# Attention in a 16-block transformer kernel: the shift of the scores moves from a second product into a row of the query stack

## What is computed

```python
q = _split_heads(queries @ Wq, h)          # h = 16 heads of 16 features
k = _split_heads(keys @ Wk, h)
v = _split_heads(values @ Wv, h)
scores = jnp.einsum('bhqd,bhkd->bhqk', q, k) / jnp.sqrt(jnp.float32(dh))
attn = jax.nn.softmax(scores, axis=-1)
y = jnp.einsum('bhqk,bhkd->bhqd', attn, v)
```

## Time and profile before

| | us |
|---|---|
| median of 3 runs | 431.51 (430.98, 431.51, 434.98) |
| the profiled execution: its own time | 433.9 |
| its span, first to last instruction | 432.0 |
| TensorE busy / VectorE busy / ScalarE busy | 344.1 / 306.4 / 248.9 |
| projection stage, until the first line 1216 | 0 to 53 |
| attention stage | 53 to about 180 |
| feed-forward stage | about 180 to 300 |
| gates and the last two layers | 300 to 432 |

### The profile page before, as it was taken

The page is one execution under the profiler, slowest core; times in us unless marked ns, Lnnn a source line. Parts: engine busy times, 40 slices in busy tenths (PEclk is TensorE's granted clock), DMA queues, the critical chain, the costliest instruction groups (busy, mean ns, idle before and its releaser), DMA issues.

```text
span 432.0 us, 9170 instructions
## 1 busy us (share of the span) xinstructions
PE 344.1 (80%) x3130; PEld 244.1 (57%) x3137; DVE 306.4 (71%) x1028; ACT 248.9 (58%) x470; POOL 185.1 (43%) x209
## 2 busy tenths in 40 slices
PE   2995698989999999824667776677489999999775
PEld 2774566767677777502445554355356666666422
DVE  3897454778898987676999999951537777787641
ACT  1564424664545545726788988874446666666520
POOL 2115200121212345149999999971004555445520
PEclk9999869999999999955999999989579999999965
DMA  7499999988476540000000000000001122212000
GB/s 242 136 281 281 273 303 289 242 167 150 95 148 112 127 71 2 1 0 0 2 1 2 0 2 1 2 0 2 0 14 27 37 51 50 50 39 39 24 25 24
DMA packets 48045, 35.78 MB, mean 83 GB/s; under 512 B 20096, under 2 KB 44032, under 8 KB 47872
## 3 DMA queue, kind: packets, MB, share of 16 engines
q1 hardware_dynamic: 48000, 35.20, 34.1%
HBM read 26.80 MB, written 8.39 MB: 81 GB/s over the span
## 4 chain that ended last, share of the span: by engine, by line
PE 53%; DVE 17%; issue 12%; ACT 5%; POOL 5%; DMA 3%; SPq 3%; DVEq 0%; POOLq 0%; ACTq 0%
PE PS L1438 6%; PE PS L1227 4%; PE PS L1216 4%; PE PS L1246 4%; DVE sm L736 4%; PE PS L1285 4%; PE PS L1428 4%; PE PS L1207 4%; PE PS L1206 4%; PE PS L1405 3%; DMA scr_k<-kpart 3%; PE PS L1423 2%; ACT pT L990 2%; SPq L315 2%; DVE sm L712 2%
## 5 line engine op out<-in xcount | busy, mean ns | idle before, releaser
L990 ACT ACTIVATE pT<-PS 128x512 f32<-128x512 f32 x64 | 36.6, 596 | 49.5 <-PE PS L1207 49.3
L605 DVE TENSOR_REDUCE negm<-PS 128x4 bf16<-128x512 f32 x64 | 42.4, 684 | 15.5 <-PE PS L1216 15.4
L434 POOL TENSOR_TENSOR sm<-sm,mhalf 128x1 f32<-128x1 f32 x16 | 11.3, 708 | 93.0 <-DVE sm L637 93.0
L450 POOL TENSOR_TENSOR kst<-kst,rows 128x1024 f32<-128x1024 f32 x16 | 37.6, 2351 | 5.0 <-ACT kst L1055 4.9
L464 POOL TENSOR_TENSOR kst<-kst,rows 128x1024 f32<-128x1024 f32 x16 | 37.8, 2365 | 0.0
L1320 PE MATMUL PS<-identf,w2f 128*128 128x128 f32 x128 | 19.2, 298 | 23.2 <-ACT w2f L1044 23.0
L1207 PE MATMUL PS<-identb,negm 128*128 128x128 bf16 x256 | 35.6, 222 | 0.0
L1227 PE MATMUL PS<-pT,vx 128*32 128x128 f32 x512 | 27.3, 287 | 5.0 <-ACT pT L990 5.0
L1320 PEld LDWEIGHTS PS<-identf,w2f 128*128 128x128 f32 x128 | 15.1, 151 | 27.7 <-ACT w2f L1044 22.4
L1438 PE MATMUL PS<-wd,xT 128*128 128x392 f32 x64 | 27.7, 560 | 1.8 <-DVE rest L884 1.8
L484 POOL TENSOR_TENSOR smd<-smd,mhalf 128x1 f32<-128x1 f32 x16 | 8.8, 550 | 44.9 <-DVE smd L915 44.9
(11 more groups left out here) (225 smaller groups left out, 1002.6 us busy)
## 6 DMA issues: line engine op xcount, KB each, us to landing
scr_q<-qpart SPq DMA_DIRECT2D x8, 384.0 KB, 4.9
scr_k<-kpart SPq DMA_DIRECT2D x8, 384.0 KB, 6.0
rows<-in_rows SPq DMA_DIRECT2D x1, 2056.0 KB, 11.3
X<-in_x SPq DMA_DIRECT2D x8, 256.0 KB, 4.7
CTXT<-in_ctxT SPq DMA_DIRECT2D x8, 256.0 KB, 4.6
cTb<-in_ctxT SPq DMA_DIRECT2D x16, 128.0 KB, 4.3
vx<-in_ctx SPq DMA_DIRECT2D x16, 128.0 KB, 2.7
out<-rest SPq DMA_DIRECT2D x16, 128.0 KB, 1.7
```

The costliest lines, as they stand in the source:

```text
L450: gp.tensor_tensor(n2[q.slot], n2[q.slot], ln2g, ALU.mult).then_inc(b_g2, 1)
L605: v.tensor_reduce(negm[f.slot % 2][:, 4 * hg:4 * hg + 4], PS[:, 2 + hg % 2, :].rearrange("p (h k) -> p h k", h=4), AX_X, ALU.max, negate=T ...
L990: s.activation(pT[:, hg, :], PS[:, hg % 2, :], ACT.Exp, scale=float(DH0) ** -0.5).then_inc(a_e, 1)
```

## The change

One row is appended to each stack, on partition 96. In the key stack it is all ones, written once by VectorE as its first four instructions. In the query stack it is the row of negated maxima of all 16 heads. For it TensorE transposes `negm` (128 by 16) at the end of the turn in which the maxima are taken, ScalarE copies the 16 by 128 result to `negmT`, and SyncE writes it by DMA as one row of 2048 values (`write_shift_row`). `shifted` is then one product of 97 rows per head.

There is one stage more: v of a block is made in the turn behind its maxima (stage m), `shifted`, the exponentials and `pv` another turn later (b is block t-2), and c, d and e are one turn later too (t-3, t-4, t-5). The loop has a turn more. On TensorE the first group of `shifted` now stands ahead of the transposes of c, and the Wo product ahead of the last `pv`; on VectorE the maxima 0 and 1 and the statistics of d stand ahead of `normalise`. SyncE's stream is a row, the stacks of the block three further on, and then the weights. The stacks still wait for the block that had their slot, which is now read a turn later.

```diff
+        negmT = [sb(f"negmT{i}", [H0, S], BF16) for i in range(2)]
...
+            def write_shift_row(at):
+                sp.wait_ge(a_n, at.b + 1)
+                sp.dma_start(qst[at.slot][STACK:STACK + 1], negmT[at.slot % 2][:]).then_inc(a_row[at.slot % 2], 16)
+
+            for x in range(NB):
+                write_shift_row(Turn(x, x % 4, x // 4))
+                if 4 <= x + 3 < NB:
+                    load_stacks(Turn(x + 3, (x + 3) % 4, (x + 3) // 4))
+                if x < 4:
+                    load_weights(x)
...
+            for i in range(4):
+                last = v.memset(kst[i][STACK:STACK + 1], 1.0)
+            last.then_inc(a_ones, 1)
...
-            def turn_a(f, _b, c, d):
-                if c:
-                    normalise(c)
-                    if c.b == 3:
-                        weight_means()
+            def turn_a(f, _m, _b, c, d):
                 if f:
                     take_max(f, 0)
                     take_max(f, 1)
                 if d:
                     bn = ln1_stats(d)
+                if c:
+                    normalise(c)
+                    if c.b == 4:
+                        weight_means()
...
-                if c and 4 <= c.b < 10:
-                    ternary_step(c.b - 4)
-                if c and c.b == 10:
+                if c and 5 <= c.b < 11:
+                    ternary_step(c.b - 5)
+                if c and c.b == 11:
                     sum_weights()
...
                 if f:
+                    act.wait_ge(a_nt, f.b + 1)
+                    if f.b >= 2:
+
+                        act.wait_ge(a_row[f.slot % 2], f.b // 2 * 16)
+                    s.activation(negmT[f.slot % 2][:], PS[0:H0, 6, 0:64].bitcast(BF16), ACT.Copy).then_inc(a_n, 1)
+                    if f.b in (5, 6):
+                        weight_sum(f.b - 5)
...
-                    pe.wait_ge(a_mx, b.b * 4 + hg + 1)
+                    if hg == 0:
+                        pe.wait_ge(a_row[b.slot % 2], 16 * (b.b // 2 + 1))
                     done(pe, a_e, b, 0, 4, hg - 1)
                     for j in range(4):
                         h = 4 * hg + j
-                        block = PS[:, hg % 2, j * 128:(j + 1) * 128]
-                        t.matmul(block, kst[b.slot][0:STACK, h, :], qst[b.slot][0:STACK, h, :], start=True, stop=False)
-                        last = t.matmul(block, negm[b.slot % 2][:, h:h + 1].to_broadcast([128, 128]), identb[:],
-                                        start=False, stop=True)
+                        last = t.matmul(PS[:, hg % 2, j * 128:(j + 1) * 128], kst[b.slot][0:STACK + 1, h, :],
+                                        qst[b.slot][0:STACK + 1, h, :], start=True, stop=True)
                     last.then_inc(a_s2, 1)
...
+                if f:
+                    pe.wait_ge(a_mx, f.b * 4 + 4)
+                    done(pe, a_n, f, 0)
+                    t.transpose(PS[0:H0, 6, 0:64].bitcast(BF16), negm[f.slot % 2][:], identb[:]).then_inc(a_nt, 1)
```

More of the change, by code:

```diff
@@ L169, in build @@
         a_ld = [sem(f"a_stacks_loaded{i}") for i in range(4)]
-        a_s1 = sem("a_scores_for_max"); a_mx = sem("a_max_taken")
+        a_row = [sem(f"a_shift_row_written{i}") for i in range(2)]; a_ones = sem("a_ones_rows_ready")
+        a_s1 = sem("a_scores_for_max"); a_mx = sem("a_max_taken"); a_nt = sem("a_max_transposed"); a_n = sem("a_maxT_ready")
         a_s2 = sem("a_scores_shifted"); a_e = sem("a_exp_ready")
@@ L441, in _ @@
             pool.wait_ge(s_rows, 16)
-            pipeline(pool, NB, 4, 4, turn_a, tail=False)
+            for t in range(NB + 1):
+                turn_a(*peeled(t, NB, 4, 5))
             def turn_b(tau, _a, _b, p, q, _c, _d, e, _f, _g):
@@ L763, in turn_b @@
                     spreads(b, d, tau)
-            pipeline(dve, NB, 4, 4, turn_a, tail=False)
-            turn_a(*peeled(NB, NB, 4, 4))
+            for t in range(NB + 2):
+                turn_a(*peeled(t, NB, 4, 5))
             first, last, before_last = Turn(0, 0, 0), Turn(NB - 1, 3, 3), Turn(NB - 2, 2, 3)
@@ L994, in turn_a @@
                     exp(1)
+                if m:
+                    act.wait_ge(a_vm, m.b + 1)
+                    done(act, a_pv, m, -1, 4)
+                    s.activation(vx[m.slot % 2][:, :, 0:DH0], PS[:, 4, 0:256].rearrange("p (h e) -> p h e", h=H0),
+                                 ACT.Copy).then_inc(a_v, 1)
+                if b:
                     if b.b == NB - 1:
@@ L1008, in turn_a @@
                 if f:
[L1009 to L1014, removed]
+                    act.wait_ge(a_nt, f.b + 1)
[4 more added lines that the diff above has]
+                        weight_sum(f.b - 5)
                 if e:
                     level(e)
-            pipeline(act, NB, 4, 5, turn_a, tail=False)
+            for t in range(NB + 1):
+                turn_a(*peeled(t, NB, 4, 6))
             def gelu(b):
@@ L1229, in pv @@
                     last.then_inc(a_pv, 1)
+                if f:
+                    pe.wait_ge(a_ld[f.slot], LOADED * (f.used + 1))
+                    for_max(0)
+                    for_max(1)
+                if m:
+                    done(pe, a_v, m, 0)
+                    for kc in range(KC):
+                        last = t.matmul(PS[:, 4, 0:256], cTb[m.slot][:, kc, :], wv[:, kc, :],
+                                        start=(kc == 0), stop=(kc == KC - 1))
+                    last.then_inc(a_vm, 1)
+                if b:
+                    shifted(0)
                 if c:
@@ L1239, in turn_a @@
                         up(Turn(1, 1, 0))
-                if f:
-                    pe.wait_ge(a_ld[f.slot], LOADED * (f.used + 1))
-                    for_max(0)
-                    for_max(1)
-                    done(pe, a_v, f, 0)
-                    for kc in range(KC):
-                        last = t.matmul(PS[:, 4, 0:256], cTb[f.slot][:, kc, :], wv[:, kc, :],
-                                        start=(kc == 0), stop=(kc == KC - 1))
-                    last.then_inc(a_vm, 1)
                 if b:
-                    shifted(0)
                     shifted(1)
@@ L1253, in turn_a @@
                         columns(Turn(0, 0, 0))
+                    pv(0)
+                if f:
+                    for_max(2)
                 if c:
@@ L1257, in turn_a @@
                     done(pe, a_x, c, 0)
-                    if isinstance(c.b, int) and c.b == 3:
+                    if c.b == 4:
                         pe.wait_ge(s_wsum, 2)
@@ L1265, in turn_a @@
                     last.then_inc(a_t2, 1)
-                if b:
-                    pv(0)
-                if f:
-                    for_max(2)
                 if b:
@@ L1287, in turn_a @@
                     last.then_inc(a_o, 1)
-            pipeline(pe, NB, 4, 3, turn_a, head=8, tail=False)
+                if b:
+                    pv(3)
+                if f:
+                    pe.wait_ge(a_mx, f.b * 4 + 4)
+                    done(pe, a_n, f, 0)
+                    t.transpose(PS[0:H0, 6, 0:64].bitcast(BF16), negm[f.slot % 2][:], identb[:]).then_inc(a_nt, 1)
+            pe.wait_ge(a_ones, 1)
+            for i in range(NB + 1):
+                turn_a(*peeled(i, NB, 4, 4))
             def turn_b(a, _b, _p, _q, c, d, _e, f, _g):
@@ L1334, in turn_b @@
                     up(a)
[L1336 removed]
+            turn_a(*peeled(NB + 1, NB, 4, 4))
             columns(Turn(1, 1, 0))
[L1338 removed]
+            turn_a(*peeled(NB + 2, NB, 4, 4))
             for tau in range(2, NB + 8):
```

36 lines of the change are left out of this document (12 added, 24 removed).

## The result

The changed kernel takes **441.12 us** (median of 4 runs, 437.72 to 442.73) beside 432.39 us of the kernel before on the same chip: ratio 1.018, 95% interval 1.0137 to 1.0223, slower by 1.8%. Its profiled execution took 440.9 us, span 439.2; before it was 433.9 and 432.0. I had forecast 431.1. All ratios leave out executions that took over 1.5% more than the fastest of the same kernel; the medians do not.

The account below looks back on a forecast made before the run. The prediction took TensorE to bound the attention turn, with VectorE next. Its terms, -15.9 + 7.5 + 2.5 + 1.5 + 4.0 = -0.4 us, gave 431.1 us from a median of 431.51; range 422 to 440.

Parts of the forecast that it names:

- Term 1: Attention loop: without 16 shift products a turn, 7.50 us falls to 6.4 plain, 7.2 ternary; about -15.9 us.
- Term 3: DMA queue: stacks lose one turn of lead and come late while weights load; 0 to 9.8 us, taken +2.5.
- Term 2: Attention's start and end: one turn more, +2.2 us in filling and 5.3 at the end; +7.5 us.
- The queue rival: Turns 4 to 7: SyncE's queue bounds, two blocks late by 4.9 us each, +9.8 for +2.5; 438.4 us; chance 0.16.
- Term 4: Last ternary step on VectorE collides with GpSimd's first scaled row in one turn; 0 to 3 us, taken +1.5.
- Term 5: Program start: VectorE's four writes of ones delay the first statistics; 0 to 6.2 us, taken +4.0.
- Short ones and a free queue: Start and DMA queue: ones are short and transfers keep up, costs fall to 0.1, 0, 0; 423.2 us; chance 0.30.
- The turn that doesn't shorten: Attention loop: VectorE and TensorE wait for each other, turns stay 7.5 us; +8.4, 439.5 us; chance 0.12.

Follow-up runs that it names:

- run 4: Kernel before without its shift products, the exponential taken of unshifted scores, nothing else changed: 425.21 us, ratio 0.9792 to the kernel before.
- run 6: Changed kernel with ScalarE's two sums over a weight moved between the last exponential and the copy of yT: 438.68 us, ratio 1.0134 to the kernel before.
- run 3: Changed kernel's deeper order with the two products of before, without ones, transposed maxima or row: 439.25 us, ratio 1.0131 to the kernel before.
- run 2: Kernel before with only the four writes of ones added at VectorE's start: 438.32 us, ratio 1.012 to the kernel before.
- run 5: Changed kernel with the row of maxima issued from ScalarE's DMA queue instead of SyncE's: 442.52 us, ratio 1.0185 to the kernel before.
- run 7: Changed kernel with the weights loaded in nine pieces of about 0.5 MB, one a turn: 436.26 us, ratio 1.0079 to the kernel before.
- run 11: Kernel before with weights in nine pieces, ScalarE's two sums moved, and scaling and rounding of weights on ScalarE: 440.31 us, ratio 1.0159 to the kernel before.
- run 1: Changed kernel with the four rows of ones written by GpSimd instead of VectorE: 434.17 us, ratio 1.0048 to the kernel before.
- run 10: Changed kernel with ones on GpSimd, sums moved and one turn later, weights in nine pieces, four of six ternary steps on ScalarE: 429.25 us, ratio 0.991.
- run 12: As run 10, but w1f issued in the first pass, other weight pieces in turns 0, 2, 4, 6, 8, 10, 11: 427.35 us, ratio 0.987.

## Why the prediction was wrong, point by point

Against the forecast of -0.4 the trace has +7.7 us at the last Wo product.

- **Term 1, the loop (-15.9): the turn right, the loop too good.** Plain 6.33 (I said 6.4), ternary 7.1 (7.2), `sum_weights` 7.5 (7.5), VectorE nearly full in the ternary ones (busy 6.7 to 6.9). That it must decide them was not right as I put it: in the old order of run 4 such a turn takes 6.74. But turns 3 to 15 took 98.6 us, not 90.1. Of the 8.5 missing, 7.0 are in the two turns with a late row (Term 3), and about 2.2 in turns 6 and 7, less 0.7 by which the other turns are shorter than forecast. Those 2.2 are the two sums on ScalarE, which I left out. I had their 1.0 us wait for the means from before and did not ask what the new order puts behind line 978: the next turn's first exponential, which comes earlier now relative to it. Run 6 shows the price, 2.6 us in its turns.
- **Term 2, one turn more (+7.5): right in kind, 1.8 short.** The filling turns took 16.0 us before turn 3, 2.9 more than before and not 2.2; from the end of turn 15 to the last Wo product it is some 6.4 more than before (16.2 us, from 173.4 to 189.6), not 5.3. Term 2 stands against the turn that Term 1 drops (13 for 14, 7.5 us), and run 3 bears out that the two nearly cancel: outside the four turns with stalls the deeper kernel loses nothing.
- **Term 3, the DMA queue (+2.5): this is the step that failed most.** I expected stacks to be late and the row only with them. No stack was; two rows were, by 2.0 and 2.1 us. And I priced a wait by its length: each cost 3.5, of it 2.0 of waiting and some 1.6 of the same products at half clock (busy 7.83 and 7.91 against 6.28), so the term was 7.0, inside its 0 to 9.8 but nearly three times what I took. I had computed that 9.4 MB take 37 us, and still counted on one late turn. The queue rival (chance 0.16) had the mechanism and came nearest: it said turns 4 to 7 and 9.8 us, priced through the stacks; the waits stand in turns 3 and 5, for the rows alone, and cost 7.0.
- **Term 4, the collision (+1.5): 0.** The two instructions began 30 ns apart, and GpSimd's was the one that grew, 3.00 to 3.90. The timeline of both:

```profile
158.79 1.21 DVE L595 TENSOR_SCALAR w2q<-w2f 128x2048 bf16<-128x2048 f32 x1
158.82 3.90 POOL L430 TENSOR_SCALAR rows<-rows,wscale 128x1024 f32<-128x1024 f32 x1
```

- **Term 5, the ones (+4.0): 5.8 between these two executions, 4.5 over nine.** The memsets start 2.14 us apart (2.15 was the working), and the first statistics stand at 9.49 (9.4). The subtraction of the 0.75 us of waiting held at first: the second statistics are 3.9 late (12.29 against 8.41). The fourth are 5.3 late (22.28 against 17.02), and the first score product 5.8. But this place scatters. In the five executions with the ones on VectorE (changed kernel, runs 2, 5, 6, 7) it stands at 58.83, 58.64, 57.33, 57.72 and 58.28, in the four without any (kernel before, runs 3, 4, 11) at 53.02, 53.56, 53.58 and 54.35: on average 58.2 and 53.6. The two profiles compared here are the latest of the one kind and the earliest of the other, so that 4.0 was nearer than 5.8 makes it look. The Trainium skill's rule in "VectorE: DVE Perf Modes", section "Zero memsets can be issued as uint32 (trn2)", one cycle per element whatever the type, agrees with the trace: 2.14 us for 2048 bf16 values is 1.04 ns each, as the f32 elements of the earlier trace rows take 1.02. No run writes another type, and the record of 1.76 us is shorter than the distance that is paid.
- **The rivals.** Short ones and a free queue: neither happened. The turn that doesn't shorten: it did shorten.

By terms, measured minus forecast: Term 1 without the rows 1.5, Term 2 1.8, Term 3 4.5, Term 4 -1.5, Term 5 1.8 (of which 1.3 is scatter of the start): 8.1, and 7.7 + 0.4 = 8.1 are to be explained. The chance of 0.28 for slower was too low: Term 3 was taken from the lower quarter of its range though my own count of bytes said that the engines would be full for 37 us, and for what I left out I had no allowance.

What stays open: when a wait ends in a slower clock. Its length doesn't decide: behind waits of 1.97 and 2.09 us (changed kernel) and 2.12 (run 7) the clock fell, behind 2.44 (run 1), 2.56 (run 6) and 2.46 (run 10) it stayed at 1.00. And how much of a row's lateness is the weights ahead of it: run 7 gained in time by smaller pieces, but the late row at 88.54 has seven transfers of stacks ahead of it too, and no run takes the weights away alone.

## What to carry to other kernels

When a change shortens a turn by adding a stage, price three things apart: the turn filled and drained (against the one that the loop has less; here the two nearly cancelled), the lead that transfers lose, and what each engine's long instructions now stand ahead of. Setup work on an engine that starts the program is paid nearly in full (4.5 of 4.7 us); give it to one that is idle there. A faster loop brings the next bound forward, so a change that loses may win once its surroundings fit it: here 441.1 became 427.4 by edits of which three together cost the old order 7 to 8 us.

## What the runs showed of the hardware

- A row of 4 KB lands 3.0 to 3.4 us after its issue from 100 to 142 us in the changed kernel (medians), and 6.0 to 10.0 behind 1 to 2 MB; behind a piece of 0.5 MB it still took 6.8 (run 10) and 8.0 (run 12, issued at 139.17). Another queue did not help (5.5 to 7.2).
- After an idle of 2.0 us TensorE went on at half clock for a time (four products 0.61 us at 78.33, 0.40 at full clock); after 1.3 and 2.4 us in run 1 it did not.
- GpSimd writes a row of 2048 values in 1.88 us; VectorE's record is 1.76, but they stand 2.14 apart from start to start.
- Beside a VectorE instruction that started 30 ns earlier, one of GpSimd took 3.90 us in place of 2.85 to 3.00, while VectorE's kept its 1.21.
